# Attention probabilities turned through device memory, one step later, and a subtraction moved to GpSimd

## The chip, the core and the metric

The kernel runs on one core of a Trainium2 chip. A core has TensorE for matrix products (PE in the profile), VectorE (DVE), ScalarE (ACT), GpSimd (POOL) and SyncE (SP), which here only issues transfers. Each engine works through its own list of instructions in order and waits on semaphores for the others. Sixteen DMA engines carry the transfers. The metric is the time of one execution on the device in microseconds; lower is better.

## The reference

Eight batches of 512 rows of 512 numbers. Cross-attention with queries that are a layer norm of `x` and with keys and values that are both the context, then a feed-forward product with 8-bit integers:

```python
q = layernorm(x)
attn = softmax(q @ ctx.T / 0.72) * mask            # mask: 0 or 1.43, an input
x1 = x + (attn @ ctx + bias) @ weights
u = layernorm(x1)
s = max(abs(u).max(-1), 1e-6) / 127
out = x1 + (round(u / s).int8() @ weight_q.T).float() * s * weight_scale + ffn_bias
```

## The kernel before

The 4096 rows are 32 tiles of 128; four tiles make a batch. A step of the program works on tile `d` and on its neighbours in the pipeline. Steps 0 to 3 are written out (`HEAD`), steps 4 to 27 are a hardware loop of three turns of eight steps (`Fori`), and steps from 28 (`TAIL`) on are written out again. Every engine runs `step(base, d)` of its own for each step, and the order of the calls in it is the engine's order of work. Nothing schedules at run time: a late operand holds the engine and all that stands behind it.

All products with float operands are made of three products of rounded parts: a `_hi` part (ScalarE writes it as a rounded copy) and a `_lo` part (the whole less the rounded part, a subtraction). So each tile needs 12 matrix instructions for `ps_scores` (queries by keys), 12 for `ps_attn` (probabilities by `vw`), 12 for `ps_vw` (context by weights, four tiles ahead), and 4 in bf16 for `ps_ffn`.

How the operands come about, for a tile n:

- Context: SyncE loads the blocks of a pair of tiles into `ctx_in` (a ring of four tiles) in `load_blocks`, for n = d + 4 when that is even, as the first act of its step. VectorE turns the 32x32 blocks (`turn_ctx`, a stream transpose into `ct_raw`) as the first act of its step d, for tile d + 4. ScalarE writes `ct_hi`, GpSimd `ct_lo`.
- Queries: ScalarE normalises (`x_norm`) and stores the rows to device memory; SyncE loads them back in blocks (`load_rows`, four transfers), VectorE turns them into `xt_raw` (`turn_x`), ScalarE writes `xt_hi`, VectorE `xt_lo`. The two together make a full transposition that costs TensorE nothing.
- Probabilities: VectorE takes the row maximum (`neg_max`), ScalarE the exponentials, VectorE multiplies by the mask (`probs`). TensorE transposes `probs` with four instructions into `ps_pt` (`turn_probs`), ScalarE copies that to `pt_hi`, and VectorE subtracts to get `pt_lo`, out of `ps_pt`.
- Integers: VectorE adds the residual (`x`, that is x1), takes its statistics, ScalarE centres (`x_neg`), VectorE finds the largest (`abs_max`) and the gains (`q_range` to `neg_gain`), ScalarE rounds in two instructions (`x_round`, `x_int`). In steps of the loop SyncE issues a DMA transpose of `x_int` into `xq_t` at the end of its step, and waits for the integers before it issues. At the end of the kernel TensorE transposes them instead, into `ps_ut`, from tile `BY_PE` on.

SyncE's step before, in order: context blocks (even steps), rows of x_norm for tile d + 1, `x_in`, `mask_in`, then the transposition of the integers of tile d - 2. These integers are ready at the end of ScalarE's step d - 1.

Of the kernel before, what the change touches and what calls it, by code (L numbers as in the profile page):

```python
# [67 lines left out]
FILLS = 9  # L68
# [16 lines left out]
BY_PE = TAIL - 2  # L85
# [67 lines left out]

def run_steps(eng, step, tail_steps=TAIL_STEPS):

    for d in range(PER_BATCH, BODY):
        step(HEAD, d)
    with eng.Fori(0, LOOPS) as pair:
        base = eng.snap(pair * BODY + LOOP_FIRST)
        for d in range(BODY):  # L160
            step(base, d)
    for d in range(tail_steps):
        step(TAIL, d)


def xattn_ffn_kernel(nc, x, ctx_rows, mask, weights, attn_bias, weight_q, weight_scale, ffn_bias, out):
# [5 lines left out]
    norm_rows = nc.dram_tensor("norm_rows", [TILES * P, D], F32, kind="Internal").ap()  # L172

    with ExitStack() as stack:
# [53 lines left out]
        xt_raw = sb("xt_raw", [P, 2, NT, P])  # L228
        ct_raw = sb("ct_raw", [P, 2, NT, P])
# [16 lines left out]
        x_sum = sb("x_sum", [P, 4])  # L246
        x_squares = sb("x_squares", [P, 4])
        sum_scale = sb("sum_scale", [P, 1])
        square_scale = sb("square_scale", [P, 1])
# [35 lines left out]
        last_ffn_banks = [ps_attn, ps_xt]  # L285

# [50 lines left out]
        norm_rows_stored = sems("norm_rows_stored", 2)  # L337
        xt_raw_ready = sem("xt_raw_ready")
# [71 lines left out]

        block = stack.enter_context(nc.Block())
# [3 lines left out]
        def _(sp):  # L415
# [53 lines left out]

            def step(base, d, row):  # L470

                n = d + 4
                if n % 2 == 0 and exists(base, n) and not is_tile(base, n, PER_BATCH) \
                        and not is_tile(base, n, PER_BATCH + 2):

                    wait_count(sp, ct_raw_ready, base, n - 4 + 2 - PER_BATCH)
                    load_blocks(ctx_in, ctx_flat, row + n * P, n, 2, ctx_loaded)
# [19 lines left out]
                if is_tile(base, d, 1):  # L497
# [4 lines left out]
                if exists(base, d - 2) and not last_batch(base):  # L502

                    wait_count(sp, x1_int_ready, base, d - 2 + 1)

                    wait_count(sp, ffn_done, base, d - 2 - 1)
                    sp.nop(nofuse=True)
                    k = slot(d, 2)
                    sp.dma_start_transpose(xq_t[:, k, :, :], x1_int[:, k, :]).then_inc(xq_t_turned[k], 16)
# [853 lines left out]
```

## Time and profile before

| what | value |
|---|---|
| time, median of 3 runs | 327.37 us (326.77 to 328.47) |
| profiled execution: its time, its span | 327.26 us, 325.1 us |
| busy: TensorE, weight loads | 316.5 us (97%), 254.8 us (78%) |
| busy: VectorE | 288.8 us (89%) |
| busy: ScalarE | 236.0 us (73%) |
| busy: GpSimd | 222.9 us (69%) |
| DMA, mean rate | 170 GB/s |
| chain that ended last: TensorE | 90% |
| largest wait of VectorE, for `ps_scores` | 9.9 us in 26 waits |

A busy share is the part of the span in which an engine had an instruction under way; instructions overlap a little, so the time that one takes of its engine is read from one start to the next. The chain that ended last follows the work back from the last instruction to what released it.

### The profile page before, as it was taken

To read this page: it belongs to the slowest core of one execution; us is meant where nothing else is said; L and a number is where in the kernel's file an instruction comes from. 1 tells how busy PE (TensorE), PEld (TensorE's weight loads), DVE (VectorE), ACT (ScalarE), POOL (GpSimd) and SP (SyncE) were. 2 spreads that over 40 slices of the span, in tenths; PEclk is the share of its full clock that TensorE was granted. 3 is DMA by queue.
4 is the path that set the end of the run, shared out by engine and by line. 5 is a ranking of instruction groups with operands and counts; after the bars stand their busy time and mean duration, and the time that the engine had idled before them with its cause. 6 is when DMAs were issued, how large, how long until landed. Compare 5 with 4: busy or idle time off the path is not lost.

```text
span 325.1 us, 6047 instructions
## 1 busy us (share of the span) xinstructions
PE 316.5 (97%) x1522; PEld 254.8 (78%) x1522; DVE 288.8 (89%) x568; ACT 236.0 (73%) x440; POOL 222.9 (69%) x359
## 2 busy tenths in 40 slices
PE   7999999999999999999999999999999999999993
PEld 7878877778877777887777788877777887777781
DVE  2888889999999999999999999999999999989986
ACT  4466778787778778777777877787787777756651
POOL 3274667677787767678776777877677787766563
PEclk9999999999999999999999999999999999999999
DMA  7997848667485855658595664748667485432002
GB/s 214 272 226 187 196 147 205 190 158 202 146 210 163 219 171 159 196 145 210 161 213 174 161 197 150 203 161 209 178 155 199 144 211 162 126 116 98 33 33 97
DMA packets 69248, 55.26 MB, mean 170 GB/s; under 512 B 21488, under 2 KB 51952, under 8 KB 69232
## 3 DMA queue, kind: packets, MB, share of 16 engines
q1 hardware_dynamic: 61312, 40.65, 49.2%
q10 hardware_dynamic: 7920, 14.42, 13.2%
q8 instruction: 6, 0.10, 0.2%
q14 instruction: 10, 0.08, 0.1%
HBM read 34.87 MB, written 16.25 MB: 157 GB/s over the span
## 4 chain that ended last, share of the span: by engine, by line
PE 90%; DMA 3%; DVE 2%; ACT 1%; SPq 1%; issue 0%; ACTq 0%
PE ps_scores L555 9%; PE ps_scores L557 9%; PE ps_scores L556 9%; PE ps_attn L557 9%; PE ps_attn L555 9%; PE ps_attn L556 9%; PE ps_vw L555 8%; PE ps_vw L557 8%; PE ps_vw L556 8%; PE ps_ffn L716 8%; PE ps_pt L547 4%; DMA x_in<-in_x_dram 2%; DMA ctx_in<-in_ctx_dram 1%; SPq L426 1%; PE ps_pt L543 1%; PE ps_ut L547 1%
## 5 line engine op out<-in xcount | busy, mean ns | idle before, releaser
L1277 POOL TENSOR_TENSOR ct_lo<-ct_raw,ct_hi 128x512 fp32r<-128x512 f32 x28 | 36.2, 1293 | 20.9 <-ACT ct_hi L768 20.9
L555 PE MATMUL ps_vw<-w_hi,ct_hi 128*128 128x512 f32 x116 | 50.5, 435 | 0.0
L555 PE MATMUL ps_attn<-vw_hi,pt_hi 128*128 128x512 f32 x124 | 48.9, 395 | 0.0
L555 PE MATMUL ps_scores<-ct_hi,xt_hi 128*128 128x512 f32 x124 | 48.7, 393 | 0.0
L557 PE MATMUL ps_attn<-vw_hi,pt_lo 128*128 128x512 f32 x124 | 48.4, 391 | 0.0
L557 PE MATMUL ps_scores<-ct_hi,xt_lo 128*128 128x512 f32 x124 | 48.3, 389 | 0.0
L556 PE MATMUL ps_scores<-ct_lo,xt_hi 128*128 128x512 f32 x124 | 48.2, 389 | 0.0
L556 PE MATMUL ps_attn<-vw_lo,pt_hi 128*128 128x512 f32 x124 | 48.2, 389 | 0.0
L1270 POOL TENSOR_TENSOR out_tile<-ffn_out,x_plus 128x512 f32<-128x512 f32 x31 | 40.3, 1299 | 8.6 <-DVE ffn_out L1020 8.6
L557 PE MATMUL ps_vw<-w_hi,ct_lo 128*128 128x512 f32 x116 | 45.4, 391 | 0.0
L556 PE MATMUL ps_vw<-w_lo,ct_hi 128*128 128x512 f32 x116 | 45.3, 390 | 0.0
L1302 POOL TENSOR_TENSOR x_in<-x_in,bias_w 128x512 f32<-128x512 f32 x32 | 41.5, 1296 | 0.7 <-issue 0.7
L1324 POOL TENSOR_TENSOR x_plus<-x,ffn_bias_wide 128x512 f32<-128x512 f32 x31 | 40.0, 1289 | 0.0
L866 ACT ACTIVATE ps_scores<-ps_scores,neg_max 128x512 f32<-128x512 f32 x32 | 21.2, 662 | 17.0 <-DVE neg_max L1117 17.0
L1289 POOL TENSOR_TENSOR scaled<-x_sum,sum_scale 128x1 f32<-128x1 f32 x27 | 5.5, 204 | 40.4 <-ACT ps_xt L786 40.4
L893 ACT ACTIVATE x_neg<-x,meanvar 128x512 f32<-128x512 f32 x32 | 23.2, 725 | 13.1 <-DVE meanvar L1184 9.5
L956 DVE STREAM_TRANSPOSE xt_raw<-x_blocks 128x512 f32<-128x512 f32 x30 | 32.6, 1088 | 0.0
L716 PE MATMUL ps_ffn<-wq_t,xq_t 128*128 128x512 bf16 x120 | 30.8, 379 | 0.7 <-ACT xq_t L833 0.7
L1117 DVE TENSOR_REDUCE neg_max<-ps_scores 128x1 f32<-128x512 f32 x32 | 22.1, 691 | 10.3 <-PE ps_scores L557 9.9
L956 DVE STREAM_TRANSPOSE ct_raw<-ctx_in 128x512 f32<-128x512 f32 x28 | 30.9, 1102 | 0.0
L778 ACT ACTIVATE x_norm<-x_in,norm 128x512 f32<-128x512 f32 x32 | 25.7, 803 | 4.7 <-POOL norm L1250 4.7
L808 ACT ACTIVATE vw_hi<-ps_vw 128x512 fp32r<-128x512 f32 x29 | 17.3, 597 | 14.3 <-PE ps_vw L557 13.8
(163 smaller groups left out, 776.6 us busy)
## 6 DMA issues: line engine op xcount, KB each, us to landing
x_in<-in_x_dram SPq DMA_DIRECT2D x32, 256.0 KB, 3.1
mask_in<-in_mask_BxSxS_fk_dram SPq DMA_DIRECT2D x32, 256.0 KB, 3.2
norm_rows<-x_norm ACTq DMA_DIRECT2D x30, 256.0 KB, 2.3
x_blocks<-norm_rows SPq DMA_DIRECT2D x120, 64.0 KB, 2.4
ctx_in<-in_ctx_dram SPq DMA_DIRECT2D x56, 128.0 KB, 3.3
out_dram<-out_tile ACTq DMA_DIRECT2D x25, 256.0 KB, 2.5
out_dram<-out_tile SPq DMA_DIRECT2D x6, 256.0 KB, 2.0
ctx_in<-in_ctx_dram SPq DMA_DIRECT2D x4, 256.0 KB, 3.9
```

The source lines that it names most:

```text
L555: nc.tensor.matmul(bank_, lhs_hi(t), rhs_hi(t), start=(t == 0), stop=False)
L556: nc.tensor.matmul(bank_, lhs_hi(t), rhs_lo(t), start=False, stop=False)
L557: last = nc.tensor.matmul(bank_, lhs_lo(t), rhs_hi(t), start=False, stop=(t == NT - 1))
L716: last = nc.tensor.matmul(ffn_bank(base, n)[:, :], xq_t[:, slot(n, 2), t, :], wq_t[:, t, :], start=(t == 0), stop=(t == NT - 1))
L778: nc.scalar.activation(x_norm[:, slot(n, 2), :], x_in[:, slot(n, 8), :], ACT.Identity, bias=norm1[:, k, 1:2], scale=norm1[:, k, 0:1]).then ...
L893: nc.scalar.activation(x1_neg[:, slot(n, 2), :], x1[:, slot(n, 2), :], ACT.Identity, bias=meanvar2[:, slot(n, 4), 0:1], scale=-1.0).then_i ...
L956: nc.vector.transpose(into.rearrange("p t (a i) -> p t a i", a=QUADS), blocks.rearrange("p (a j t) -> p t a j", a=QUADS, t=NT)).then_inc(r ...
L1117: nc.vector.tensor_reduce(col(neg_max, d), ps_scores[:, :], AX_X, ALU.max, negate=True).then_inc(neg_max_ready, 1)
L1270: nc.gpsimd.tensor_tensor(out_tile[:, slot(n, 2), :], ffn_out[:, slot(n, 2), :], x1_plus[:, slot(n, 2), :], ALU.add).then_inc(out_ready, 1)
L1277: nc.gpsimd.tensor_tensor(ct_lo[:, batch_of(n), :, j * P:(j + 1) * P], ct_raw[:, slot(n, 2), :, :], ct_hi[:, batch_of(n), :, j * P:(j + 1) ...
L1302: nc.gpsimd.tensor_tensor(x_in[:, slot(d, 8), :], x_in[:, slot(d, 8), :], bias_w[:, :], ALU.add).then_inc(x_plus_ready, 1)
L1324: nc.gpsimd.tensor_tensor(into, x1[:, slot(n, 2), :], ffn_bias_wide[:, :], ALU.add).then_inc(x1_plus_ready, 1)
```

## The change

Between step 3 and step 28 (`is_middle`: all steps of the loop, and step 3):

- TensorE's four transposes of `probs` are gone. VectorE writes `probs` in another order of columns, SyncE stores the tile to device memory (`prob_rows`, 256 KB) and loads it back in four transfers into `p_blocks` (which lies where `wq_rows` was); VectorE turns the blocks into `pt_raw` with a stream transpose, and `pt_hi` and `pt_lo` are made from `pt_raw`. `ps_ut` is free and becomes a second bank for `ps_vw`.
- All that follows comes a step later: the attention product of tile d - 2 in step d, the integers and the feed-forward product of tile d - 3, and the output of tile d - 4.
- `xt_lo` is made by GpSimd; the residual, its statistics (`bn_stats`, `bn_aggr`) and the row sums' reciprocals stay on VectorE in a new order. GpSimd has one small operation fewer in `norm_factors`.
- SyncE's step is now: rows of tile d + 1, store of `probs` of tile d - 1, `x_in`, `mask_in`, context blocks (even steps), load of `probs` of tile d - 1, transposition of the integers of tile d - 3.
- In `TAIL`, one more attention and feed-forward product stand in the written-out steps, TensorE transposes the integers of three tiles instead of six, and the last tile's integers are rounded, transposed and copied in halves.

The core of the diff:

```diff
-BY_PE = TAIL - 2
+BY_PE = TAIL + 1
+BOUNCED_FROM = PER_BATCH - 1
+POOL_LO_FROM = PER_BATCH - 1
...
+def is_middle(base, d):
+    return not isinstance(base, int) or base + d == PER_BATCH - 1
...
+    prob_rows = nc.dram_tensor("prob_rows", [TILES * P, ROWS], F32, kind="Internal").ap()
...
+        def vw_bank(base, n):
+            if isinstance(base, int) and base + n < PER_BATCH + 3:
+                return ps_vw
+            return [ps_vw, ps_ut][slot(n, 2)]
...
+        p_blocks = flat(wq_rows[:, :, :]).bitcast(F32).rearrange("p (k d) -> p k d", k=2)
```

SyncE:

```diff
+            def store_probs(base, n, row):
+                wait_count(sp, probs_ready, base, n + 1)
+                sp.dma_start(prob_rows[bass.ds(row, P), :], probs[:, slot(n, 2), :]) \
+                    .then_inc(prob_rows_stored[slot(n, 2)], 16)
+            def load_probs(base, n, row):
+                quads = prob_rows[bass.ds(row, P), :].rearrange("(a i) d -> i a d", i=BLOCK)
+                wait_bounced(sp, prob_rows_stored, base, n)
+                for b in range(QUADS):
+                    blocks = p_blocks[b * BLOCK:(b + 1) * BLOCK, slot(n, 2), :]
+                    sp.dma_start(blocks.rearrange("i (a c) -> i a c", a=QUADS),
+                                 quads[:, :, b * P:(b + 1) * P]).then_inc(p_blocks_loaded[slot(n, 2)], 16)
+            def turn_integers(base, n):
+                wait_count(sp, x1_int_ready, base, n + 1)
+                sp.nop(nofuse=True)
+                k = slot(n, 2)
+                sp.dma_start_transpose(xq_t[:, k, :, :], x1_int[:, k, :]).then_inc(xq_t_turned[k], 16)
             def step(base, d, row):
-                n = d + 4
-                if n % 2 == 0 and exists(base, n) and not is_tile(base, n, PER_BATCH) \
-                        and not is_tile(base, n, PER_BATCH + 2):
-                    wait_count(sp, ct_raw_ready, base, n - 4 + 2 - PER_BATCH)
-                    load_blocks(ctx_in, ctx_flat, row + n * P, n, 2, ctx_loaded)
+                bounced = in_loop(base) or is_tile(base, d, TAIL)
                 n = d + 1
...
                 if exists(base, n) and not is_tile(base, n, 1):
                     load_rows(base, n, row + n * P)
+                if bounced:
+                    store_probs(base, d - 1, row + (d - 1) * P)
                 n = d + 4
...
                     load_x(row + n * P, slot(n, 8))
...
                     load_mask(row + n * P, slot(n, 4))
+                n = d + 4
+                if n % 2 == 0 and exists(base, n) and not is_tile(base, n, PER_BATCH) \
+                        and not is_tile(base, n, PER_BATCH + 2):
+                    wait_count(sp, ct_raw_ready, base, n - 4 + 2 - PER_BATCH)
+                    load_blocks(ctx_in, ctx_flat, row + n * P, n, 2, ctx_loaded)
...
-                if exists(base, d - 2) and not last_batch(base):
-                    wait_count(sp, x1_int_ready, base, d - 2 + 1)
-                    wait_count(sp, ffn_done, base, d - 2 - 1)
...
+                if bounced:
+                    load_probs(base, d - 1, row + (d - 1) * P)
+                n = d - 3
+                if exists(base, n) and (in_loop(base) or base + n < BY_PE):
+                    turn_integers(base, n)
```

TensorE:

```diff
+                if is_middle(base, d):
+                    if in_loop(base):
+                        attend(d - 2)
+                    next_vw(d + 4)
+                    feed_forward(d - 3)
+                elif is_tile(base, d, TAIL):
+                    attend(d - 2)
+                    feed_forward(d - 3)
+                    turn_probs(d)
```

ScalarE:

```diff
+                if is_middle(base, d):
+                    split_next_ctx(d + 4)
+                    if in_loop(base):
+                        round_integers(d - 3)
+                        store_integers(d - 3)
+                    exponentials()
...
+                    split_next_x()
+                    add_up_x(base, d + 4)
+                    if in_loop(base):
+                        split_late_vw(d + 3)
+                        centre(d - 2)
+                        split_bounced_probs(d - 1)
+                    add_up_squares(base, d + 4)
+                    normalise(base, d + 3)
+                    store_rows(base, d + 3, (base + d + 3) * P)
+                    return
```

VectorE:

```diff
+                def turn_probs(n):
+                    wait_bounced(dve, p_blocks_loaded, base, n, QUADS)
+                    turn_blocks(pt_raw[:, :, :], p_blocks[:, slot(n, 2), :], pt_raw_ready)
+                def split_bounced_probs(n):
+                    wait_count(dve, pt_hi_ready, base, n + 1)
+                    lo_part(flat(pt_lo[:, slot(n, 2), :, :]), flat(pt_raw[:, :, :]),
+                            flat(pt_hi[:, slot(n, 2), :, :]), pt_lo_ready)
+                def masked():
...
+                    if is_middle(base, d):
+                        into = into.rearrange("p (c t) -> p t c", t=NT)
+                        exps = exps.rearrange("p (t c) -> p t c", t=NT)
+                        mask_tile = mask_tile.rearrange("p (t c) -> p t c", t=NT)
+                    nc.vector.tensor_tensor(into, exps, mask_tile, ALU.mult).then_inc(probs_ready, 1)
...
+                if is_middle(base, d):
+                    turn_ctx(base, d + 4)
+                    if in_loop(base):
+                        gains(d - 3)
+                        scale_ffn(d - 4)
+                    else:
+                        dve.wait_ge(wscale_loaded, 16)
+                    highest()
+                    turn_x(base, d + 1)
+                    masked()
+                    if in_loop(base):
+                        residual(d - 2)
+                        wait_count(dve, stats2_ready, base, d - 2 + 1)
+                    invert_sum()
+                    if in_loop(base):
+                        nc.vector.bn_aggr(meanvar2[:, slot(d - 2, 4), :],
+                                          stats2[:, slot(d - 2, 4), :]).then_inc(meanvar2_ready, 1)
+                        turn_probs(d - 1)
+                        split_vw(base, d + 3, vw_bank(base, d + 3))
+                        largest(d - 2)
+                        split_bounced_probs(d - 1)
+                    return
```

GpSimd:

```diff
+                def split_next_x():
+                    n = d + 1
+                    wait_count(pool, xt_hi_ready, base, n + 1)
+                    nc.gpsimd.tensor_tensor(flat(xt_lo[:, slot(n, 2), :, :]), flat(xt_raw[:, slot(n, 2), :, :]),
+                                            flat(xt_hi[:, slot(n, 2), :, :].bitcast(F32)),
+                                            ALU.subtract).then_inc(xt_lo_pool_ready, 1)
+                if is_middle(base, d):
+                    if in_loop(base):
+                        inverse_deviation(d - 3)
+                    split_next_ctx(d + 4)
+                    if in_loop(base):
+                        add_up(d - 4)
+                    add_bias()
+                    split_next_x()
+                    next_mean()
+                    norm_factors(base, d + 3)
+                    if in_loop(base):
+                        add_ffn_bias(d - 2)
+                    return
```

## Rows read from the trace of the kernel before

**Rows 1.** Windows of 20 us: busy us (instructions) by engine, clock, DMA share, GB/s.

```profile
160.00:180.00 20.00, 20.00 (x94) 16.07 (x93) 18.48 (x39) 15.84 (x30) 15.10 (x24) 1.00 0.64 175
```

**Rows 2.** Timeline of TensorE, one step: start us, us, instruction.

```profile
152.77 0.39 PE L555 MATMUL ps_attn<-vw_hi,pt_hi 128*128 128x512 f32 x1
...
155.50 0.60 PE L547 MATMUL ps_pt<-identity,probs 128*128 128x128 f32 x4
155.93 1.03 PE L716 MATMUL ps_ffn<-wq_t,xq_t 128*128 128x512 bf16 x4
...
164.99 0.60 PE L547 MATMUL ps_pt<-identity,probs 128*128 128x128 f32 x4
```

**Rows 3.** Timeline of VectorE, one step; idle time ahead in brackets.

```profile
160.98 1.11 DVE L956 STREAM_TRANSPOSE ct_raw<-ctx_in 128x512 f32<-128x512 f32 x1
162.46 0.69 DVE L1117 TENSOR_REDUCE neg_max<-ps_scores 128x1 f32<-128x512 f32 x1 [0.37 <-PE ps_scores L557]
163.07 1.08 DVE L956 STREAM_TRANSPOSE xt_raw<-x_blocks 128x512 f32<-128x512 f32 x1
164.08 0.65 DVE L1139 TENSOR_TENSOR probs<-ps_scores,mask_in 128x512 f32<-128x512 f32 x1
164.85 0.69 DVE L940 TENSOR_TENSOR xt_lo<-xt_raw,xt_hi 128x512 fp32r<-128x512 f32 x1
...
167.12 0.72 DVE L1020 SCALAR_TENSOR_TENSOR ffn_out<-ps_ffn,x_scale,wscale_wide 128x512 f32<-128x512 f32 x1
167.76 0.68 DVE L940 TENSOR_TENSOR pt_lo<-ps_pt,pt_hi 128x512 fp32r<-128x512 f32 x1
...
169.13 0.21 DVE L1040 TENSOR_SCALAR q_range<-abs_max,rstd 128x1 f32<-128x1 f32 x1
...
169.88 0.69 DVE L940 TENSOR_TENSOR vw_lo<-ps_vw,vw_hi 128x512 fp32r<-128x512 f32 x1
```

**Rows 4.** Timeline of ScalarE, the two instructions that make the integers.

```profile
160.42 0.82 ACT L839 ACTIVATE x_round<-x_neg,round_magic,neg_gain 128x512 f32<-128x512 f32 x1
161.26 0.63 ACT L851 ACTIVATE x_int<-x_round 128x512 bf16<-128x512 f32 x1
```

**Rows 5.** Timeline of SyncE's queue: start of the issue, us spent issuing.

```profile
161.98 1.20 SPq L509 DMA_TRANSPOSE xq_t<-x_int  x1
163.38 2.05 SPq L426 DMA_DIRECT2D ctx_in<-in_ctx_dram  x4
165.52 1.90 SPq L435 DMA_DIRECT2D x_blocks<-norm_rows  x4
167.51 0.38 SPq L417 DMA_DIRECT2D x_in<-in_x_dram  x1
168.06 0.35 SPq L439 DMA_DIRECT2D mask_in<-in_mask_BxSxS_fk_dram  x1
```

**Rows 6.** Landing of the 44 context loads issued between 55 and 280 us.

```profile
DMA to landing us min/median/max: 2.4/3.3/4.7
```

**Rows 7.** VectorE's line 1102 (ns min/median/max) and GpSimd's timeline over its first run.

```profile
L1102 DVE TENSOR_TENSOR ct_raw<-ct_raw x2: 425/810/1196, 320.8 to 322.5; 128x256 f32<-128x256 f32 x2
...
320.48 1.26 POOL L1270 TENSOR_TENSOR out_tile<-ffn_out,x_plus 128x512 f32<-128x512 f32 x1 [0.31 <-DVE ffn_out L1020]
```

**Rows 8.** Timeline of GpSimd: two adds, and its small operations.

```profile
150.08 1.29 POOL L1324 TENSOR_TENSOR x_plus<-x,ffn_bias_wide 128x512 f32<-128x512 f32 x1
151.33 1.30 POOL L1270 TENSOR_TENSOR out_tile<-ffn_out,x_plus 128x512 f32<-128x512 f32 x1
...
156.10 0.19 POOL L1289 TENSOR_TENSOR scaled<-x_sum,sum_scale 128x1 f32<-128x1 f32 x1 [1.47 <-ACT ps_xt L786]
...
157.55 1.29 POOL L1302 TENSOR_TENSOR x_in<-x_in,bias_w 128x512 f32<-128x512 f32 x1
```

**Rows 9.** VectorE's timeline: first instruction of step 3 and of step 28.

```profile
47.48 1.10 DVE L956 STREAM_TRANSPOSE ct_raw<-ctx_in 128x512 f32<-128x512 f32 x1
...
284.46 1.10 DVE L956 STREAM_TRANSPOSE xt_raw<-x_blocks 128x512 f32<-128x512 f32 x1
```

More of the change, by code:

```diff
@@ L516, in step @@
                             .then_inc(last_stored, 16)
-                elif last_batch(base) and not is_tile(base, n, TAIL - PER_BATCH):
+                elif last_batch(base):
                     wait_count(sp, out_ready, base, n + 1)
@@ L642, in turn_integers @@
                     if is_tile(base, n, LAST):
-                        pe.wait_ge(last_x1_int_ready, 1)
-                    else:
-                        wait_count(pe, x1_int_ready, base, n + 1)
+                        pe.wait_ge(xq_t_ready, base + n - BY_PE)
+                        for h in range(2):
+                            pe.wait_ge(last_x1_int_ready, h + 1)
+                            for t in range(h * NT // 2, (h + 1) * NT // 2):
+                                turned = nc.tensor.transpose(last_ut_banks[h][:, :].bitcast(BF16)[:, t * P:(t + 1) * P],
+                                                             x1_int[:, slot(n, 2), t * P:(t + 1) * P],
+                                                             identity16[:, :])
+                            turned.then_inc(ut_done, 1)
+                        return
+                    wait_count(pe, x1_int_ready, base, n + 1)
                     if not is_tile(base, n, BY_PE):
@@ L898, in step @@
                     centre(d - 1)
-                if last_batch(base) and d > 0 and not is_tile(base, d - 2, LAST):
+                if last_batch(base) and d > 1 and not is_tile(base, d - 2, LAST):
                     round_integers(d - 2)
@@ new lines, in step @@
+                if is_tile(base, d, TAIL):
+                    turn_x(base, d + 1)
+                    gains(d - 3)
+                    scale_ffn(d - 4)
+                    highest()
+                    masked()
+                    invert_sum()
+                    residual(d - 2)
+                    average(d - 2)
+                    turn_probs(d - 1)
+                    split_vw(base, d + 3, vw_bank(base, d + 3))
+                    largest(d - 2)
+                    split_bounced_probs(d - 1)
+                    split_probs(d)
+                    return
@@ L1113, in step @@
+                if is_tile(base, d, 0):
+                    turn_ctx(base, d + 4)
+                if exists(base, d + 1) and last_batch(base):
+                    turn_x(base, d + 1)
+                if is_tile(base, d - 1, TAIL):
+                    gains(d - 3)
+                    scale_ffn(d - 4)
+                elif is_tile(base, d - 2, TAIL):
+                    gains(d - 3)
+                elif is_tile(base, d, LAST):
                     largest(d - 2)
                 if exists(base, d):
-                    wait_count(dve, scores_done, base, d + 1)
@@ L1157, in step @@
                     x_mean_var(d + 3)
-                if last_batch(base) and d > 0 and exists(base, d):
-                    scale_ffn(d - 3)
+                if last_batch(base) and d > 1 and exists(base, d):
+                    scale_ffn(d - 4)
+                if is_tile(base, d - 1, TAIL):
+                    residual(d - 2)
+                    average(d - 2)
+                    largest(d - 2)
                 if is_tile(base, d - 1, LAST):
@@ L1196, in step @@
                         split_vw(base, d + t, first_vw_banks[t])
-                if exists(base, d - 1) and not last_batch(base):
-                    quantisation(d - 1)
-                if is_tile(base, d, 0):
                     turn_ctx(base, d + 6)
+                elif exists(base, d - 1) and not last_batch(base):
+                    largest(d - 1)
+                if is_tile(base, d, 2):
+                    gains(d - 2)
                 if exists(base, d + 4):
-                    split_vw(base, d + 4, ps_vw)
-                if is_tile(base, d - 2, 0):
-                    scale_ffn(d - 2)
+                    split_vw(base, d + 4, vw_bank(base, d + 4))
                 if is_tile(base, d - 2, LAST):
@@ L1226, in _ @@
             pool.wait_ge(identity_ready, 1)
+            for k in range(2):
+                nc.gpsimd.memset(stored_start[:, k:k + 1], 0.0).then_inc(out_stored[k], 16)
             nc.gpsimd.tensor_copy(identity16[:, :], identity[:, :]).then_inc(identity16_ready, 1)
```

366 lines of the change are left out of this document (230 added, 136 removed).

## The prediction

> **What bounds the kernel now.** I read the windows first: in any 20 us of the loop TensorE is busy for all 20, VectorE for 18.5, ScalarE for 15.8, GpSimd for 15.1, and DMA share is 0.64 [rows 1]. A busy engine need not be the bound, so TensorE's timeline comes next. A step is the distance between two transpositions of the probabilities: 164.99 - 155.50 = 9.49 us [rows 2]. The attention product takes 155.50 - 152.77 = 2.73 us for 12 instructions, the transposition 155.93 - 155.50 = 0.43, and 9.49 - 0.43 - 3 x 2.73 = 0.87 is left for the feed-forward product: issue back to back, no gap. The reader is to see that TensorE sets the pace, and that taking four transposes away can give 0.43 us a step, 9.06 in place of 9.49, if nothing else takes more than 9.06.
>
> **VectorE, the next in line.** I add its step from start to start [rows 3]: turn context 1.01 (as the next turn, 163.07 to 164.08), maximum 0.61, turn x 1.01, mask 0.61 (its 0.77 has a gap), 2.91 from `xt_lo` through `ffn_out` to `pt_lo`, that and the largest 0.61 each, gains 0.75, `vw_lo` 0.61: 8.7 us of 9.49, with 0.37 idle ahead of the maximum. The change takes `xt_lo` (0.61) off it and puts a stream transpose (1.01) on it: 9.1 us. So VectorE has no slack left beside TensorE's 9.06, and whatever it waits for lengthens the step.
>
> **The wait that the change adds: context blocks.** VectorE's step begins with the turn of context tile d + 4. SyncE loads that pair in its own step d, for even d. I ask when SyncE comes to it. Before, the integers are ready at 161.26 + 0.63 = 161.89 [rows 4], SyncE transposes them at 161.98 and issues the context at 163.38, 2.4 us after VectorE's step began at 160.98 and a step ahead of the turn that needs it, one step of 9.49 later, at 170.5 [rows 3, 5]. The last of four issues starts about 1.6 later; with a median landing of 3.3 us [rows 6] the pair is there at 168.3, 2.2 us early.
>
> After, two things move the issue back. SyncE's step d + 1 starts after the transposition of the integers of tile d - 3, and ScalarE makes these only in step d, after it has split context tile d + 4, with gains that VectorE makes after it has turned that tile. And rows, store, `x_in` and `mask_in` now stand ahead of the context. From VectorE's first instruction of an odd step d:
>
> - turn 1.01 and gains 0.66 (0.75 less a gap): 1.7 us;
> - `x_round` and `x_int`, 161.89 - 160.42 = 1.5 [rows 4]: 3.2;
> - transposition up to the next issue, 163.38 - 161.89 = 1.5: 4.7;
> - rows, 167.51 - 165.52 = 2.0: 6.7;
> - store, `x_in`, `mask_in` at 168.06 - 167.51 = 0.55 each [rows 5]: 8.3;
> - last context issue 1.6 later, landing 3.3: 13.2 us.
>
> VectorE could start its next step at 9.1 and waits till 13.2. No engine can get past this: the turn is first in VectorE's list, behind it stand the other 16 of its instructions; ScalarE waits for `ct_raw`, GpSimd for `ct_hi`, TensorE for `ct_lo` before its product for tile d + 4. The chain runs from turn to turn through SyncE's list and closes on itself, so no buffer makes up for it. The pair serves two tiles: only the way from an odd to an even step is longer. Its bounds: with 2.4 us to land and issues as fast as the issue times alone (1.9 for rows, 0.38 each for the three) 12 us, still over 9.49; with 4.7 to land 14.6. I take the median.
>
> The other transfers: `prob_rows` adds 256 KB out and 256 KB in a step. The store goes out at 6.7, after `probs` (ready near 4.7); in a step without context blocks the load goes out about 9.2, lands near 13.5 and is needed by VectorE at 9.1 + 6.2 = 15.3, so it costs nothing, and in the longer step there is more room. DMA share of 0.64 in 9.49 us leaves room for 0.5 MB beside 1.7 MB (175 GB/s x 9.49 us). If that cover goes, context lands later too, which the 4.7 holds.
>
> **GpSimd and `pt_lo`.** In the last 5 us GpSimd adds a tile (320.48 to 321.74) while VectorE's line 1102, which reads two tensors in SBUF, runs: 1196 ns against 425 in its other run [rows 7]. It ended at 322.03, 0.29 after GpSimd's. `pt_lo` reads two SBUF tensors from now on (it read PSUM), and `xt_lo` no longer runs on VectorE. GpSimd's step, from the start of VectorE's: `ct_hi` is there at 1.8; four adds of 1.25 [rows 8] to 6.8; small operations, 157.55 - 156.10 = 1.45 less one of 0.2, to 8.0; the `ffn_bias` add to 9.3. VectorE comes to `pt_lo` near 8.5, inside that last add, and ends it at about 9.3 + 0.5 = 9.8. So an even step takes 9.75 rather than 9.1. In odd steps the wait for the context hides it. Bounds: 0, if it falls beside the add, and 1.25.
>
> The Trainium skill (GPSIMD Engine Reference, section Specifications) says that GpSimd shares its SBUF interfaces with VectorE and contends with it in instructions with two SBUF inputs. By that rule, the trace agrees. The same notes (VectorE: DVE Perf Modes, section on the TRN2 errata) give an instruction out of SBUF 62 cycles less than one out of PSUM; by the page `pt_lo` would save 0.065 us x 25 = 1.6 us. In this trace `pt_lo` out of PSUM takes 0.68 and `xt_lo` out of SBUF 0.69 [rows 3], so the sum has nothing for it.
>
> Other edits. `probs` written with a stride: no row of an elementwise write with one; nothing below, and above 0.4 (a turn, 1.01, less an elementwise 0.61), in even steps only: up to 5 us; I take 0, since it works on the same 512 elements. `ps_vw` in two banks takes a wait away that cost TensorE nothing. `ffn_out` of tile 0 leaves the start: -0.6. At the end one attention and one feed-forward product more, 2.73 + 0.87, less three bf16 transpositions and the halves of the last tile, together about 1: +2.6.
>
> **The sum.** VectorE's step 3 starts at 47.48 and its step 28 at 284.46: 237.0 us [rows 9]. After: step 3 has no attention, and step 4's context follows `probs` (3.3), three issues (1.65), 1.6 and 3.3: 9.9. Then twelve even steps at 9.75 = 117.0, eleven odd ones at 13.2 = 145.2, and step 27, after which no context comes, 9.75: 281.9, or +44.9. With -0.6 and +2.6 the span goes from 325.1 to 372.0. The profiled execution's time is 2.2 above its span, and 0.1 below the median, so 374.
>
> **The rivals.** What the measurement of this kernel can tell from no change is about 0.5%.
>
> - Forecast, context late and `pt_lo` behind GpSimd: 374 (365 to 388). Chance 0.52.
> - Context late, but `pt_lo` clear of GpSimd's add (0.65 us less in thirteen steps, 8.5): 365. It decides if GpSimd's chain shifts by 0.5 us earlier or 0.8 later. 0.28.
> - The other side: the context is there in time. Then TensorE's 9.06 rules: step 3 about 6.5, 24 x 9.06 = 217.4, so 223.9 for 237.0, and -0.6 + 2.6: 316. It needs the context chain under 9.06 us in place of 13.2, so SyncE's issues shorter by over 4 us, or a turn that works on a pair that came a step earlier. For it speaks that all transfers before were early; against it every link above. 0.07.
> - Context in time, `pt_lo` behind GpSimd: 6.5 + 24 x 9.75 = 240.5, so 333. 0.07.
> - TensorE loses its clock in the new waits. The granted clock is 1.00 in the loop [rows 1], the full 2.4 GHz; a wait of TensorE of some 3.7 us in every other step has no like in this trace. At half speed a whole step would be 18.1 against 13.2 and 9.75: at most 24 x 18.1 = 434, or some 158 us over the forecast's 276 for these steps; most of it would be hidden, as TensorE has 4.8 us to spare in two steps, so more likely 390 to 400. 0.04. The Trainium skill (TensorE: Matmul & The Clock Gate, Part 1) says that the array's clock falls to 1.2 GHz when it is idle; no run here shows it.
>
> The remaining 0.02 is no change. The likeliest two hold 0.80, so the range is 356 to 390, from the 365 with a chain 0.8 us shorter (11 x 0.8 = 9) to the 374 with the slowest landing, 1.4 us more (11 x 1.4 = 15). Slower: 0.52 + 0.28 + 0.07 + 0.04 = 0.91; same 0.02; faster 0.07.
>
> **What would show it.** Chain of waits: VectorE's context turn (`ct_raw`) waits for the `ctx_in` transfer 11 or 12 times, 4 us each, and that wait tops the list. SyncE's timeline: context issues about 8.3 us after the turn of the odd step. TensorE: no `ps_pt` in the loop, idle ahead of `ps_vw`, busy share near 82%. Steps alternate between 13 and 9.8 us. `pt_lo` takes 1.3 us in place of 0.68. Wrong would be: steps of even length, context transfers issued before the integers' transposition, or `pt_lo` at 0.7 with GpSimd's adds elsewhere.

## The result: 416.4 us, 27% slower

The changed kernel takes 416.42 us (median of 4, 414.22 to 417.80), the kernel before 327.92 beside it: ratio 1.269, 95% interval 1.262 to 1.277. The profiled execution took 417.32 us, its span 415.5. I forecast slower, 374 us in a range of 356 to 390: right direction, 42 us too low.

The page of the changed kernel: totals, three rows in 40 slices with the granted clock, and the chain that ended last.

```profile
span 415.5 us, 6094 instructions
PE 339.9 (82%) x1410; PEld 258.7 (62%) x1410; DVE 314.5 (76%) x566; ACT 226.1 (54%) x438; POOL 265.8 (64%) x362
...
PE   8989698959689595795959969489594996979694
...
DVE  4888709959497792986959699197794969986776
...
PEclk9999979979989799698998969979899798999799
...
issue 24%; DVE 19%; POOL 17%; SPq 13%; DMA 13%; PE 7%; ACT 6%; POOLq 0%; DVEq 0%; ACTq 0%
```

In the loop of the kernel before TensorE was full and no engine under 0.75 [rows 1]; here all are idle for a good part: something is waited for. Its waits (engine and line, who ended it: us in total, times, longest):

```profile
ACT ct_hi L862 <- DVE ct_raw L1111: 104.3, 27, 9.5
POOL ct_lo L1513 <- ACT ct_hi L862: 97.1, 27, 9.7
DVE ct_raw L1111 <- DMA ctx_in<-in_ctx_dram: 70.5, 12, 10.0
PE ps_vw L621 <- POOL ct_lo L1513: 57.5, 12, 7.4
```

The two longest are ScalarE and GpSimd, which wait for VectorE's context turn and for each other behind it. The one that starts the chain is the third: the forecast wait for `ctx_in`, twelve times, but 5.9 us each rather than 4. VectorE's timeline over one odd step and into the even one:

```profile
175.72 1.08 DVE L1111 STREAM_TRANSPOSE ct_raw<-ctx_in 128x512 f32<-128x512 f32 x1
176.73 0.17 DVE L1243 TENSOR_SCALAR q_range<-abs_max,rstd 128x1 f32<-128x1 f32 x1
...
179.57 1.08 DVE L1222 TENSOR_TENSOR probs<-ps_scores,mask_in 128x512 f32<-128x512 f32 x1
...
184.38 1.46 DVE L1095 TENSOR_TENSOR pt_lo<-pt_raw,pt_hi 128x512 fp32r<-128x512 f32 x1
190.62 1.08 DVE L1111 STREAM_TRANSPOSE ct_raw<-ctx_in 128x512 f32<-128x512 f32 x1 [4.78 <-DMA ctx_in<-in_ctx_dram]
```

and SyncE's queue in the same step (start, us spent issuing), which answers to [rows 5]:

```profile
178.94 1.20 SPq L532 DMA_TRANSPOSE xq_t<-x_int  x1
180.23 2.02 SPq L477 DMA_DIRECT2D x_blocks<-norm_rows  x4
182.43 0.38 SPq L515 DMA_DIRECT2D prob_rows<-probs  x1
183.01 0.35 SPq L459 DMA_DIRECT2D x_in<-in_x_dram  x1
183.47 0.40 SPq L481 DMA_DIRECT2D mask_in<-in_mask_BxSxS_fk_dram  x1
183.96 1.90 SPq L468 DMA_DIRECT2D ctx_in<-in_ctx_dram  x4
```

The first context issue is 183.96 - 175.72 = 8.24 us after the turn; I had 8.3. What follows is longer: 1.9 of issues and 4.8 until VectorE can go on, so 14.9 for the step where I had 13.2. In the timeline of the changed kernel VectorE's `ct_raw` starts step 3 at 48.62 and its `xt_raw` step 28 at 363.26. The whole difference, in the spans (415.5 against my 372.0):

| stretch | forecast | measured | excess |
|---|---|---|---|
| start to step 3 | 46.9 | 48.6 | 1.7 |
| step 3 to 4 | 9.9 | 13.7 | 3.8 |
| eleven odd-to-even steps | 145.2 | 171.3 | 26.1 |
| thirteen others | 126.8 | 129.7 | 2.9 |
| step 28 to the end | 43.2 | 52.2 | 9.0 |

(The first row varies by itself: with the same code up to there, e14 reaches step 3 at 47.1 and e9 at 51.1.) Two of the eleven steps take 18.2 and 18.5 us, those across the turns of the loop, where SyncE goes back to the first instruction of its loop body. SyncE's queue at one of them stands still for 3.6 us behind the transposition:

```profile
150.72 1.21 SPq L532 DMA_TRANSPOSE xq_t<-x_int  x1
155.52 1.85 SPq L477 DMA_DIRECT2D x_blocks<-norm_rows  x4
```

### The profile page after: what moved, and what is told of

Its sections match the earlier page's. It is cut to its first block, busy times and chain, and to the rows that moved or that the text cites. A ratio compares the mean times of both kernels' runs of the same rounds, so it can differ in the third digit from the quotient of the medians.

```text
span 415.5 us, 6094 instructions
## 1 busy us (share of the span) xinstructions
PE 339.9 (82%) x1410; PEld 258.7 (62%) x1410; DVE 314.5 (76%) x566; ACT 226.1 (54%) x438; POOL 265.8 (64%) x362
## 3 DMA queue, kind: packets, MB, share of 16 engines
q1 hardware_dynamic: 81088, 54.43, 48.4%
## 4 chain that ended last, share of the span: by engine, by line
issue 24%; DVE 19%; POOL 17%; SPq 13%; DMA 13%; PE 7%; ACT 6%; POOLq 0%; DVEq 0%; ACTq 0%
DMA ctx_in<-in_ctx_dram 10%; SPq L477 4%; SPq L468 4%; POOL x_in L1540 3%; POOL out_tile L1506 3%; POOL x_plus L1564 3%; DVE pt_lo L1095 3%; SPq L532 3%; DVE ct_raw L1111 2%; DVE xt_raw L1111 2%; DMA x_in<-in_x_dram 2%; DVE pt_raw L1111 2%; ACT x_round L942 2%; POOL xt_lo L1521 2%; ACT x_int L954 2%
## 5 line engine op out<-in xcount | busy, mean ns | idle before, releaser
L1111 DVE STREAM_TRANSPOSE ct_raw<-ctx_in 128x512 f32<-128x512 f32 x28 | 30.3, 1081 | 70.5 <-DMA ctx_in<-in_ctx_dram 70.5
L621 PE MATMUL ps_vw<-w_hi,ct_hi 128*128 128x512 f32 x64 | 35.7, 558 | 57.5 <-POOL ct_lo L1513 57.5
L862 ACT ACTIVATE ct_hi<-ct_raw 128x512 fp32r<-128x512 f32 x28 | 17.7, 631 | 104.4 <-DVE ct_raw L1111 104.3
L621 PEld LDWEIGHTS ps_vw<-w_hi,ct_hi 128*128 128x128 f32 x64 | 17.0, 266 | 66.2 <-POOL ct_lo L1513 45.0
L621 PE MATMUL ps_scores<-ct_hi,xt_hi 128*128 128x512 f32 x124 | 54.7, 441 | 0.1
L1521 POOL TENSOR_TENSOR xt_lo<-xt_raw,xt_hi 128x512 fp32r<-128x512 f32 x29 | 37.5, 1293 | 12.7 <-ACT xt_hi L897 11.6
L897 ACT ACTIVATE xt_hi<-xt_raw 128x512 fp32r<-128x512 f32 x30 | 19.0, 632 | 28.7 <-POOL out_tile L1506 26.5
L1095 DVE TENSOR_TENSOR pt_lo<-pt_raw,pt_hi 128x512 fp32r<-128x512 f32 x25 | 34.1, 1365 | 0.0
L1222 DVE TENSOR_TENSOR probs<-ps_scores,mask_in 128x512 f32<-128x512 f32 x32 | 31.8, 995 | 2.6 <-ACT ps_scores L965 2.5
L622 PE MATMUL ps_vw<-w_lo,ct_hi 128*128 128x512 f32 x64 | 33.5, 523 | 0.0
L623 PE MATMUL ps_vw<-w_hi,ct_lo 128*128 128x512 f32 x64 | 32.9, 514 | 0.0
```

Source lines behind the costliest of these rows:

```text
L621: nc.tensor.matmul(bank_, lhs_hi(t), rhs_hi(t), start=(t == 0), stop=False)
L622: nc.tensor.matmul(bank_, lhs_hi(t), rhs_lo(t), start=False, stop=False)
L623: last = nc.tensor.matmul(bank_, lhs_lo(t), rhs_hi(t), start=False, stop=(t == NT - 1))
L1095: nc.vector.tensor_tensor(lo, whole, hi.bitcast(F32), ALU.subtract).then_inc(ready, 1)
L1111: nc.vector.transpose(into.rearrange("p t (a i) -> p t a i", a=QUADS), blocks.rearrange("p (a j t) -> p t a j", a=QUADS, t=NT)).then_inc(r ...
L1222: nc.vector.tensor_tensor(into, exps, mask_tile, ALU.mult).then_inc(probs_ready, 1)
```

## Experiments

The kernel before ran beside each, with medians from 326.3 to 327.2 us; the intervals of the ratios are of 95%.

### e1, e2: is it the place of the context load?

```
# e1: load_blocks(ctx_in, ...) for n = d + 4 ahead of load_rows
# e2: the same place, but n = d + 5 in odd steps:
+ n = d + 5
+ if n % 2 == 0 and exists(base, n) and ...:
+     load_blocks(ctx_in, ctx_flat, last_row if in_loop(base) and d == BODY - 1
+                 else row + n * P, n, 2, ctx_loaded)
```

> The changed kernel with one edit: the load of the context pair stands first in SyncE's step again, ahead of the rows, the stored probabilities, x_in and mask_in, but still behind the transposition of the integers in the step before. My theory (the pair is late because of what SyncE issues ahead of it): the odd-to-even step falls from 14.9 us to the 3.2 us at which the transposition is issued, 1.3 of it, 1.9 of four issues and 3.5 to 4.1 of landing, 10 to 10.5; twelve such steps give 52 to 58 us, so 416 becomes 362 (355 to 370). Rival (the 8 transfers of the bounce and the clock make every step long, wherever the context stands): the wait for the context moves to the blocks of the probabilities and the time stays above 395.

Measured: 356.74 us, ratio 1.093 (1.088 to 1.098). The even-to-odd and odd-to-even steps are both 10.0, but for 12.5 at the loop's start, 12.4 and 12.9 at its turns and one of 10.5.

> The changed kernel with one edit: the context pair is loaded a step earlier, first in SyncE's odd step (the tile of d+5; the last one, which no tile needs, reads the first rows again). Then it can't be late. My theory: every step is the even one, 9.7 to 10.0 us, bound by VectorE with pt_lo at 1.37 us and the strided probabilities at 1.0 us; 25 steps of 9.85 are 246 us against 314.6 from step 3 to step 28, so 416 becomes 348 (342 to 356), about the 20 us above the kernel before that the tail (11.6) and 25 steps of 0.4 make. Rival one (ordering is all of it, VectorE isn't the bound): PE's 9.06, 328 to 336. Rival two (the blocks of the probabilities are next late, they are issued behind everything): 365 or more.

Measured: 354.92 us, ratio 1.087 (1.079 to 1.095). One load moved gives back 60 of the 89 us: its place in SyncE's list is the main cause, and the rival with the bounce's transfers falls. That e1 and e2 are alike says that coming first in the step is early enough.

### e3, e4, e6, e7: what makes the step of 10.0 us

With the context in time VectorE is the bound: in e2 it is busy for 9.86 of 9.96 us from 190.22 to 200.18. Two of its operations are longer than before. First the end of e2's step, VectorE and GpSimd:

```profile
198.42 1.29 POOL L1565 TENSOR_TENSOR x_plus<-x,ffn_bias_wide 128x512 f32<-128x512 f32 x1
199.68 0.63 POOL L1547 TENSOR_TENSOR var_eps<-meanvar,eps 128x1 f32<-128x1 f32 x1
...
198.79 1.47 DVE L1096 TENSOR_TENSOR pt_lo<-pt_raw,pt_hi 128x512 fp32r<-128x512 f32 x1
200.18 1.09 DVE L1112 STREAM_TRANSPOSE ct_raw<-ctx_in 128x512 f32<-128x512 f32 x1
```

`pt_lo` ends 0.55 us after GpSimd's add does; the line in [rows 7] ended 0.29 after. The add keeps its 1.29 us, but GpSimd's next operation, on a single column, takes 0.63 us and ends with `pt_lo`; in e4, below, it takes 0.20. So in this meeting VectorE is held by the add, and then GpSimd by the subtraction.

e4 gives `xt_lo` back to VectorE:

```
-  # gpsimd, split_next_x()
+  masked(); split_next_x()   # vector, same operands
```

> e2 with xt_lo back on VectorE, behind the probabilities; the rest of the change stays. Theory (the two engines collide at a subtraction whose operands are all in SBUF): pt_lo falls from 1.37 to 0.68 us once GpSimd has 1.3 us of work less beside it, and VectorE gets 0.69 for xt_lo: its own sum is unchanged, and the time is e2's within 3 us. If pt_lo stays near 1.3 (it is GpSimd's add of the bias that it meets, not xt_lo), VectorE has 0.69 more in each of 25 steps: up to 17 us slower than e2.

Measured: 362.09 us, ratio 1.108 (1.104 to 1.112), steps of 10.7: slower than e2 by 7 us, between the two expectations. The line of `pt_lo` in e4 (ns min/median/max):

```profile
L1096 DVE TENSOR_TENSOR pt_lo<-pt_raw,pt_hi x25: 670/680/1001, 63.9 to 319.6; 128x512 fp32r<-128x512 f32 x25
```

It is 0.68 with the same SBUF operands, because GpSimd's `x_plus` (189.79 to 191.09) ends before `pt_lo` begins (192.25). But VectorE waits 0.6 to 0.7 us a step for `xt_hi` ahead of `xt_lo`, which I hadn't counted, and that wait is the whole difference to e2: 10.7 less 0.7 is e2's 10.0. In this place of VectorE's list `xt_lo` is better on GpSimd; another place wasn't tried.

e6 leaves it there and turns the probabilities into a bank of PSUM:

```
+ def turned_probs(base):
+     return ps_pt[...] if in_loop(base) else pt_raw[:, :, :]
- turn_blocks(pt_raw[:, :, :], p_blocks[...], pt_raw_ready)
+ turn_blocks(turned_probs(base), p_blocks[...], pt_raw_ready)
```

> e2 (context a step early) with one more edit: in the loop VectorE's transposition of the probabilities writes a bank of PSUM that is free there instead of an SBUF tile, and pt_lo subtracts from that bank. Theory (pt_lo takes twice as long only when GpSimd works beside it and its operands are all in SBUF): pt_lo falls from 1.4 to 0.68 us beside the same GpSimd add, each step from 10.0 to 9.3 us, 25 steps give 17: 338 (334 to 343). Rival one (the doubling is a matter of time beside GpSimd alone): pt_lo stays at 1.4 and the time at 355. Rival two (TensorE, busy 9.8 of 10.0 us by the records, is as much the bound): pt_lo falls and the time stays above 349.

Measured: 347.47 us, ratio 1.063 (1.057 to 1.068). Line of `pt_lo` (ns min/median/max), then by the timeline GpSimd's add and VectorE's `pt_lo` in one step of e6:

```profile
L1100 DVE TENSOR_TENSOR pt_lo<-ps_pt,pt_hi x31: 658/679/695, 26.5 to 329.8; 128x512 fp32r<-128x512 f32 x31
```

```profile
183.28 1.30 POOL L1569 TENSOR_TENSOR x_plus<-x,ffn_bias_wide 128x512 f32<-128x512 f32 x1
...
183.68 0.69 DVE L1100 TENSOR_TENSOR pt_lo<-ps_pt,pt_hi 128x512 fp32r<-128x512 f32 x1
```

0.69 in the middle of the same add. So the doubling needs both: GpSimd at work and both operands in SBUF. Steps of 9.16 occur now (that is VectorE's bare sum), but of the 22 steps from 5 to 27 eight take about 9.2, eight 9.4 to 9.9 and six 10.1 to 12.0, and the time fell by 7.5 us, not 17. VectorE waits for the probabilities' blocks 8 times (6.9 us) and TensorE 18.8 us for `xq_t`, both of which SyncE issues: the bound begins to go over to SyncE's queue.

The second long operation is `probs`. In the change it is written to every fourth element. e3 writes it in order and reads both operands in steps of 128 elements instead; e7 (on e6) takes the reordering away.

```
 into.rearrange("p (c t) -> p t c", t=NT)      # the change
 exps.rearrange("p (t c) -> p c t", t=NT)      # e3 (and the mask), into "p (c t) -> p c t"
 pass                                          # e7
```

> e2 with one more edit: VectorE's product that makes the probabilities writes its row in order and reads the exponentials and the mask with the stride, rather than the other way round (the result is the same). If the stride costs only on the written side, the product falls from 1.0 to 0.66 us and each of 25 steps by 0.35 where VectorE is the bound: 8 us under e2 (6 to 10). If reading with the stride costs as much: e2's time within 2 us. If VectorE isn't the bound in e2: within 2 us though the product is shorter.

Measured: 353.81 us, ratio 1.082 (1.078 to 1.086).

> e6 with one more edit: the probabilities are written in the order of their columns, without the stride; the columns then reach the attention in another order than the rows of the context, so this kernel doesn't compute the reference's output, and its time alone is read. VectorE's product falls from 1.07 to 0.66 us as in the kernel before. If VectorE still bounds e6, each step loses 0.3 to 0.4, 8 to 10 us under e6; if TensorE bounds it by then (9.06 us of work in a step by my prediction), 3 to 6; if something else does, nothing.

Measured: 346.52 us, ratio 1.061 (1.057 to 1.065). The line of `probs` in e3, and in e7:

```profile
L1223 DVE TENSOR_TENSOR probs<-ps_scores,mask_in x32: 658/1086/1105, 20.0 to 335.2; 128x512 f32<-128x512 f32 x32
```

```profile
L1225 DVE TENSOR_TENSOR probs<-ps_scores,mask_in x32: 647/691/693, 19.6 to 323.1; 128x512 f32<-128x512 f32 x32
```

The reordering costs 0.4 us in either form, my upper bound. Taking it away shortened the operation; the time isn't told apart from e6's, which fits a bound that is no longer VectorE.

### e5: issues or bytes ahead of the context?

```
  load_rows; store_probs
+ load_blocks(ctx_in, ...)
  load_x; load_mask
- load_blocks(ctx_in, ...)
```

> The changed kernel with one edit: within SyncE's step the context pair is issued ahead of x_in and mask_in instead of behind them; it stays behind the transposition, the rows and the stored probabilities. It asks how much of the late landing is the issuing and how much the 512 KB that stand ahead in the DMA queue. If only the issuing counts (my prediction's terms: two issues of 0.5 us), the odd-to-even step falls by 1.0, twelve times: 404 (400 to 408). If the context lands late because the bytes ahead of it must move first (512 KB at the 240 GB/s of the busy stretches are 2.1 us), it falls by up to 3.1: 379 (375 to 390).

Measured: 392.59 us, ratio 1.201 (1.198 to 1.204): 24 us less than the changed kernel, 2.0 on average in each of twelve places, between the two. 1.0 is the issues; the rest fits the landing of the context (us from issue to landing, min/median/max, of those issued between 55 and 350 us, in the changed kernel and then in e5):

```profile
DMA to landing us min/median/max: 3.3/4.1/5.8
```

```profile
DMA to landing us min/median/max: 2.3/3.0/5.6
```

So the 512 KB of `x_in` and `mask_in` ahead cost 1.1 us of landing. Before it was 3.3 [rows 6], which I took over. VectorE goes on when the last of the pair's four loads has landed; taken alone, that one needs 4.95 us at the median of the twelve places in the changed kernel, 4.05 in e5 and 3.5 in the kernel before.

### e8, e9: SyncE at the turn of the loop

```
- with sp.Fori(0, LOOPS) as pair:
+ with nc.Fori(0, LOOPS, engines=[sp.engine], hint_back_edge=True) as pair:
```

e8 is on e6, e9 on the changed kernel.

> e6 with one more edit: SyncE's loop is given a hint ahead of its closing branch, so that the loop's first instructions are fetched before the branch. Theory (SyncE's gap of 3.6 us between the transposition and the rows at the two turns of the loop is the fetching of its code): the gap goes, the steps at the turns fall from 11.3 to the usual length, 2 to 5 us under e6. If the gap is something else (the register arithmetic at the loop's head, a wait), the time is e6's within 1.5 us.

Measured: 340.45 us, ratio 1.045 (1.039 to 1.052), 7 us under e6.

> The changed kernel with one edit, the hint of e8 ahead of the closing branch of SyncE's loop; the context stays late. Theory: of what the changed kernel takes beyond my prediction, 7 us are SyncE's two gaps of 3.6 us at the turns of the loop, which the kernel before hid because SyncE ran ahead of the others there, and which the late context puts on the path: the two steps of 18.2 and 18.5 us become 14.9 like the others, 416 becomes 409 (406 to 411). Rival (the two long steps have another cause, or the time comes back in the next step): 416 within 1.5.

Measured: 410.90 us, ratio 1.252 (1.244 to 1.260), apart from 1.262 to 1.277. SyncE's queue at the same turn in e9, then in the kernel before:

```profile
152.74 1.20 SPq L532 DMA_TRANSPOSE xq_t<-x_int  x1
154.72 1.83 SPq L477 DMA_DIRECT2D x_blocks<-norm_rows  x4
```

```profile
123.95 1.20 SPq L509 DMA_TRANSPOSE xq_t<-x_int  x1
125.86 1.87 SPq L426 DMA_DIRECT2D ctx_in<-in_ctx_dram  x4
```

In e9 it is 0.8 us from the end of one to the next, for 3.6, and the two steps take 15.2. So the gap is the way back to the loop's head, which the hint shortens, and it is worth 5.5 us by the medians where SyncE is on the path (6.3 by the two steps). The kernel before has a gap of only 0.7 at both of its turns, without the hint. The pages count the packets of the queue that brings instructions, in the kernel before, in the changed kernel and in e9:

```profile
q14 instruction: 10, 0.08, 0.1%
```

```profile
q14 instruction: 21, 0.17, 0.2%
```

```profile
q14 instruction: 10, 0.08, 0.1%
```

In the changed kernel one such packet moves in each of the two gaps (near 153.8 and 255 us); the kernel before and e9 have none at either turn. So the long gap came with the change, and the rows fit SyncE waiting there for instructions. The change lengthened the body of SyncE's loop from 72 issues to 112 in eight steps; that this length decides is likely, but no run varied it alone.

### e13b, e14: TensorE's clock

The changed kernel by windows around one wait (busy us by engine, granted clock, DMA share, GB/s):

```profile
162.00:167.00 5.00, 0.00 (x0) 0.00 (x0) 1.23 (x3) 0.15 (x1) 0.00 (x0) 0.98 0.74 144
167.00:169.00 2.00, 0.04 (x1) 0.05 (x1) 2.00 (x6) 1.97 (x4) 1.44 (x2) 0.50 0.00 0
169.00:174.00 5.00, 5.00 (x13) 3.77 (x14) 4.93 (x9) 3.55 (x9) 4.67 (x8) 0.53 0.58 163
```

From 162 to 167 us TensorE has no product and the clock is still 0.98; from 167 to 169 it is 0.50 (1.2 GHz), and the product of `vw` behind it takes 5.0 us, for the 2.73 of twelve such instructions at the full clock. As the Trainium skill has it (TensorE: Matmul & The Clock Gate, Part 1), an idle array falls to 1.2 GHz; the trace agrees. Does it cost time?

```
  attend(d - 2)
+ if d % 2 == 0:
+     warm_up(ps_pt, 48)      # e14: 22
  next_vw(d + 4)
```

> The changed kernel with one edit: in each even step of the loop TensorE gets 48 products of ones (128x128, some 0.12 us each, 5.8 us) into a bank that nobody reads there, ahead of the wait for the late tile of context, so that it is idle for one or two us there and not for seven. Rival (TensorE loses its clock in the new waits and the following products at half speed are part of the 89 us): the clock stays at its full level and the time falls by up to the 2.3 us that the first product of vw loses there, twelve times, to 390. Theory (the engine has slack behind the late context, VectorE waits 0.6 us in the whole loop for scores): the clock rises from 0.914 to above 0.97 and the time stays at 416 within 4.

Measured: 457.85 us, ratio 1.399 (1.392 to 1.405), clock 0.989. It doesn't decide: the filling stood on the path (10.9 us where I had meant 5.8).

> As e13b with 22 products of ones instead of 48: each is two passes of 0.11 us in the trace of e13b, so 48 were 10.9 us and not 5.8 and stood on the path themselves; 22 are 5.0 us, in a wait of 7. Rival (TensorE loses its clock in the new waits and the products at half speed behind them are part of the excess): with the clock full there the time falls by up to the 2.3 us that a product of vw loses at half speed, twelve times, to 390. Theory (the engine has slack behind the late context, VectorE waits 0.6 us in the whole loop for scores): the clock rises from 0.914 to above 0.96 and the time stays at 416 within 4.

Measured: 417.80 us, ratio 1.273 (1.268 to 1.278), clock 0.967, TensorE's wait ahead of `ps_vw` down from 57.5 to 9.5 us. Some 60% of the lost clock is back and the time is the same, as is VectorE's wait for the context (71.7 us for 70.5). So the lost clock isn't seen to cost anything here; TensorE has slack behind the late context.

### e10, e11, e12b: how far does it go

e10 (on e8) issues the tail's rows a step earlier. e11 puts SyncE's step in another order. e12b moves the context pair behind the transposition, two steps ahead, and a feed-forward product of the tail behind the next scores.

```
  # SyncE's step from e11 on
  store_probs(d - 1); load_rows(d + 1); load_x(d + 4); load_mask(d + 2)
  load_probs(d - 1)
  # e11: context pair of d + 5 here, odd d
  turn_integers(d - 3)
  # e12b: context pair of d + 6 here instead, even d
```

> e8 with one more edit: in the last four steps SyncE issues the rows of the next tile but one ahead of the transposition and of the store of out_tile, instead of a step later behind that store. Theory: the wait of 2.4 us of xt_raw for its blocks in the tail goes, and the scores behind it start earlier: 3 us under e8, 337 (335 to 339). Rival (the tail is bound by its chain of ScalarE, VectorE and TensorE, the rows were not the last to come): within 1 us of e8.

Measured: 338.92 us, ratio 1.035 (1.027 to 1.042). The interval overlaps with e8's: not told apart. VectorE's late wait for its rows is gone, other waits have taken its place, and from step 28 to the end it is 51.6 us for e8's 51.9: the rival was right.

> e10 with one more edit, the order of SyncE's step: the stored probabilities first, then the rows, x_in and mask_in, then the load of the probabilities, then (odd steps) the context pair, then the transposition. The landing of the store is then covered by 2.8 us of issues rather than 0.8. Theory (SyncE's queue, with some 9 of 9.4 us of each step taken, sets when the integers are turned, and TensorE waits 15 us in all for them): the waits for xq_t and for the blocks of the probabilities go, the step falls from 9.5 on average to VectorE's 9.2, 7 us under e10: 330 (327 to 334). Rival one (TensorE is the bound in those steps): within 2 us of e10. Rival two (the rows now come too late for xt_raw): slower than e10 by 5 or more.

Measured: 337.54 us, ratio 1.031 (1.028 to 1.034), no different. Even and odd steps now fall apart: 9.16, which is VectorE's sum, and mostly 10.0 and more, it seems because the context's four issues stand ahead of a transposition that TensorE waits for. e12b puts that to the test.

> e11 with two more edits. SyncE issues the context pair of d+6 at the end of the even step, behind the transposition, so that nothing of it stands ahead of a transposition that TensorE waits for; and in the first step of the tail TensorE takes the product of tile d-3 with the quantised weight behind the next tile's scores instead of ahead of the turned probabilities, where it waited 4.0 us for its integers. Theory: the odd step falls from 10.0 to the 9.2 us of the even one (VectorE's sum), 10 us in twelve pairs, and the tail loses 2.5 to 3: 325 (322 to 329), as fast as the kernel before. Rival (SyncE's sum of a pair, some 18 of 18.4 us, still holds one of the two steps): 330 to 335.

Measured: 334.36 us, ratio 1.023 (1.018 to 1.029). The rival was right: steps of about 9.2 and 9.5. SyncE's queue over a step in e12b:

```profile
191.57 1.20 SPq L536 DMA_TRANSPOSE xq_t<-x_int  x1
193.04 2.04 SPq L472 DMA_DIRECT2D ctx_in<-in_ctx_dram  x4
195.25 0.37 SPq L519 DMA_DIRECT2D prob_rows<-probs  x1
195.80 1.81 SPq L481 DMA_DIRECT2D x_blocks<-norm_rows  x4
197.81 0.35 SPq L463 DMA_DIRECT2D x_in<-in_x_dram  x1
198.26 0.38 SPq L485 DMA_DIRECT2D mask_in<-in_mask_BxSxS_fk_dram  x1
198.73 1.98 SPq L528 DMA_DIRECT2D wq_rows<-prob_rows  x4
200.97 1.20 SPq L536 DMA_TRANSPOSE xq_t<-x_int  x1
```

One issue follows on another for 9.4 us, the length of the longer step. From step 5 to step 27 (22 steps) `ct_raw` goes from 65.81 to 272.46, 9.39 a step for 9.50 before (66.09 to 274.98): at its best the idea gains 2 us in the loop. From step 28 on it takes 48.4 us for 40.6, and loses them. No version here beats the kernel before.

## Why the prediction was wrong

- **The mechanism was right.** The context late behind rows, store, `x_in`, `mask_in` and the transposition; the first issue 8.24 us after the turn for 8.3 forecast; VectorE's wait for it 12 times, behind only the two waits that hang on it; steps alternating; `ps_pt` gone from the loop; TensorE busy 82%. e1 and e2 show the cause.
- **The landing was mis-sized**: "I take the median" of 3.3 us. It is a median of single loads issued before `x_in` and `mask_in`, while VectorE waits for the last of four, behind them. In the step shown the four take 3.6, 3.9, 4.1 and 5.1 us, so it is 8.24 + 1.6 + 5.1 = 14.9, beyond my bound of 14.6 for the slowest landing. Of the median's 4.95 for 3.3, 0.2 is the choice of the last load (3.5 in the kernel before), 0.9 goes with `x_in` and `mask_in` (e5), and for the other 0.55 I have no run. Over nine usual steps (14.95 for 13.2) it makes 16 us. In step 3 to 4 it makes 1.7 of the 3.8; the other 2.1 is that the first context issue comes 7.0 us after the turn for my 4.95, since the store stood behind a transposition and the rows.
- **A place put at nothing: the turn of the loop.** The sum has its steps like all others. I looked at what the change adds to SyncE's step and not at what the longer list does to the way back: the gap there grew from 0.7 to 3.6 us. That and the longer landing make the two long steps; e9 gave back 5.5 us.
- **The even step: 9.97 for 9.75, by errors that cancel.** VectorE's sum without stride and collision is 9.16 - 0.4 = 8.8 (e7's shortest step is 8.86), not 9.1; the stride, taken at 0, is 0.4; `pt_lo` loses 0.8 beside GpSimd, not 0.65. That 9.97 lies so close to the forecast is luck. I also let `pt_lo` end 0.5 us after the add, where my own row had 0.29; it is 0.55. e4 and e6 show the collision as it was argued; the Trainium skill (GPSIMD Engine Reference, section Specifications) names two SBUF inputs as its condition, and e6 bears that out.
- **The tail was mis-sized: +2.6 for +11.6.** I counted TensorE's products and not the chain from step to step. VectorE's longest waits there are 2.34 us for the rows of the last tile, behind `out_tile`'s store, and 2.69 for its scores. Taking the first away (e10) gave 0.3 us, so it wasn't the bound. From step 28 to the end it is 51.9 in e8, 51.6 in e10, 50.5 in e11 and 48.4 in e12b, for 52.2 in the changed kernel: the order of SyncE's list and the place of the feed-forward product hold some 3 us. How the other 7.8 over the kernel before divide was not tried.
- **The rival of the clock** was weighed right in kind, since the clock did fall, and e14 shows no cost of it here. Its price had a slip: the forecast for those 24 steps is 272 us, not 276.
- **The range** reached to the slowest landing alone. The tail, the turn and the landing go the same way, each by 7 to 20 us: it should have added them.

## What to carry to other kernels

When a load is moved behind other entries of one engine's DMA list, follow the list until it closes on itself: the first engine that waits for a transfer whose issue waits for that same engine sets the step. And a landing time belongs to its place in the queue: take it with the bytes that will stand ahead. When a load comes in several transfers, take the last of them. When an edit lengthens a queue's loop body, look at the gap at the loop's turn, and count the queue's own issues as an engine's busy time.

## What I had not expected of the hardware

- SyncE stands still for 3.6 us where its loop of 112 issues turns back, 0.8 with a branch hint (e9), and 0.7 without one in the kernel before, whose loop has 72.
- A 128x512 f32 product on VectorE takes 1.08 us for 0.69, whether it writes every fourth element (e2) or reads in steps of 128 elements (e3).
- A subtraction on VectorE with both inputs in SBUF takes 1.44 us at the median beside a GpSimd add, 0.68 without one (e2, e4), and 0.68 beside it with one input in PSUM (e6). The Trainium skill (VectorE: DVE Perf Modes, section on the TRN2 errata) has 62 cycles less for SBUF than for PSUM; here 0.680 and 0.679 are the same.
- A product of 128x128 f32 ones is two instructions of some 0.115 us in the trace (e14: 44 in 5.07 us for 22 products).
